# Entry of the experts in a vision tower: the shared expert's products moved ahead into the second norm, the router and the top-k

## The reference

```python
def _L0_ffn_ref(hidden_states, gate_w, Wg, Wu, Wd, Sg, Su, Sd):
    ...
    logits = flat_x @ gate_w.T
    scores = jax.nn.softmax(logits, axis=-1).T
    topk_weight, topk_idx = jax.lax.top_k(scores, C)
    xg = flat_x[topk_idx]
    ...
    sg = hidden_states @ Sg.T
    su = hidden_states @ Su.T
    shared = jax.nn.gelu(sg, approximate=False) * su @ Sd.T
    return out + shared
```

## Time and profile before

| | us |
|---|---|
| median of 3 runs | 865.48 (864.29 to 866.86) |
| the profiled execution's own time | 864.54 |
| its span, first to last instruction | 862.7 |
| PE busy (share of the span) | 798.5 (93%) |
| DVE busy | 642.3 (74%) |
| ACT busy | 462.2 (54%) |
| POOL busy | 256.9 (30%) |

### The profile page before, as it was taken

One profiled execution on the slowest core, in us unless ns is written; L12 is line 12 of the kernel. 1 busy time (PEld: TensorE's weight loads), 2 busy tenths in 40 slices (PEclk: granted clock), 3 DMA queues, 4 the chain that ended last, 5 costly groups with the idle time before them and its releaser, 6 DMA issues.

```text
span 862.7 us, 15969 instructions
## 1 busy us (share of the span) xinstructions
PE 798.5 (93%) x5736; PEld 731.1 (85%) x5736; DVE 642.3 (74%) x1285; ACT 462.2 (54%) x820; POOL 256.9 (30%) x297
## 2 busy tenths in 40 slices
PE   5889899999999997999999999989999998979698
PEld 4788769999999987898898979879897997969466
DVE  5696593877788768778778787877878787765686
ACT  3385314433333345776775777677567667725421
POOL 0002100411111101641654364164436516422232
PEclk9899799999999998899999999999999999988889
DMA  5000936988888702000210210021021002200000
GB/s 180 1 1 4 401 95 233 336 318 319 315 318 319 285 1 101 26 13 13 99 36 12 67 67 1 12 97 36 12 79 55 0 12 97 101 1 1 0 1 29
DMA packets 18289, 88.33 MB, mean 102 GB/s; under 512 B 3121, under 2 KB 7473, under 8 KB 12241
## 3 DMA queue, kind: packets, MB, share of 16 engines
q1 hardware_dynamic: 18256, 87.90, 28.8%
HBM read 85.05 MB, written 2.84 MB: 102 GB/s over the span
## 4 chain that ended last, share of the span: by engine, by line
PE 42%; issue 27%; POOL 18%; DVE 9%; ACT 3%; DMA 1%; POOLq 0%; SPq 0%; DVEq 0%; ACTq 0%
PE bank L1084 13%; POOL W_L L1903 6%; PE bank L1121 5%; POOL arena L1888 4%; POOL HF_L L1947 4%; PE bank L1226 3%; POOL WQKV_L L1903 2%; PE bank L770 2%; PE bank L724 2%; PE bank L1130 2%; POOL SQ L1917 2%; PE bank L1402 2%; PE bank L1067 1%; PE bank L872 1%; DVE CN L1991 1%
## 5 line engine op out<-in xcount | busy, mean ns | idle before, releaser
L1084 PE MATMUL bank<-arena 128*128 (+1 forms) x1024 | 117.9, 274 | 0.5 <-ACT arena L1646 0.5
L1084 PEld LDWEIGHTS bank<-arena 128*128 128x128 f32 x1024 | 117.4, 192 | 0.7 <-ACT arena L1646 0.7
L1888 POOL TENSOR_TENSOR arena<-arena,srec 111x456 f32<-111x456 f32 x56 | 52.4, 963 | 129.4 <-DVE srec L2047 129.4
L770 PE MATMUL bank<-XHL,W_H 128*128 128x296 f32 x384 | 90.2, 314 | 0.0
L770 PE MATMUL bank<-XHL,WQKV_H 128*128 128x296 f32 x288 | 73.1, 327 | 6.3 <-DVE XHL L2488 4.9
L1947 POOL TENSOR_TENSOR HF_L<-arena,HF_H 128x296 fp32r<-128x296 f32 x48 | 43.8, 935 | 111.5 <-ACT HF_H L1803 111.5
L1903 POOL TENSOR_TENSOR W_L<-LW,W_H 128x256 fp32r<-128x256 f32 x96 | 70.1, 772 | 18.9 <-ACT W_H L1689 18.9
L770 PEld LDWEIGHTS bank<-XHL,W_H 128*128 128x128 f32 x384 | 66.0, 194 | 1.2 <-DVE XHL L2488 1.2
L1803 ACT ACTIVATE arena<-bank,vec 128x296 f32<-128x296 f32 x96 | 48.8, 509 | 23.0 <-PE bank L770 22.4
L2059 DVE TENSOR_SCALAR OB<-bank,lvec 96x148 f32<-96x148 f32 x144 | 51.2, 368 | 12.8 <-PE bank L840 10.4
L770 PEld LDWEIGHTS bank<-XHL,WQKV_H 128*128 128x128 f32 x288 | 49.3, 192 | 13.2 <-DVE XHL L2488 8.0
(11 more groups left out here) (260 smaller groups left out, 2080.9 us busy)
## 6 DMA issues: line engine op xcount, KB each, us to landing
arena<-ew_in SPq DMA_DIRECT2D x16, 2048.0 KB, 9.3
arena<-ew_in SPq DMA_DIRECT2D x16, 1024.0 KB, 6.7
LW<-lw_in SPq DMA_DIRECT2D x12, 1024.0 KB, 4.9
arena<-route SPq DMA_DIRECT2D x32, 185.0 KB, 3.4
LW<-lw_in SPq DMA_DIRECT2D x6, 768.0 KB, 4.4
fp_weights<-arena SPq DMA_DIRECT2D x1, 2048.0 KB, 6.4
arena<-fp_weights SPq DMA_DIRECT2D x1, 2048.0 KB, 7.1
arena<-patches_in SPq DMA_DIRECT2D x2, 864.0 KB, 8.3
```

What stands on the lines that cost most here:

```text
L770: last = mm(o, w, x, start=(i == 0), stop=(i == len(pairs) - 1))
L1084: last = mm(o[:, m * CAP:(m + 1) * CAP], w[:, kc, mi * P:(mi + 1) * P], xg(kc, e), start=(kc == 0), stop=(kc == C - 1))
L1888: nc.gpsimd.tensor_tensor(v, v, srec[0:QROWS, s:s + 2, :].unsqueeze(3).to_broadcast([QROWS, 2, C * JH, KEYS]), ALU.mult).then_inc(p_ready, 1)
```

## The change

- The shared weights move within `LW`. Gate and up (`Ws_gu`) get a place that is free as soon as ACT has cast the last attention weight (`wo_cast`), and are loaded then. The down weights (`Ws_d`) are loaded once PE is through with the first attention products, on a semaphore of their own.
- On PE the gate half of pair 0 goes between the norm's mean and its variance, the up half of pair 0 between the norm's broadcast and the logits of tiles 2 to 4, and pair 1 between the logits and the score transposes. Logits of tiles 0 and 1 go behind the variance.
- All token transposes go behind the score transposes and write banks 6 and 7, in three groups with one copy each on ACT.
- Pairs 2 to 7 follow, with down products 0, 1 and 2 between them. The banks of the pairs are (2, 3), (4, 5), then (2, 3) and (0, 1) by turns. The score transposes write banks 0 and 1.
- On ACT the table of Exp is loaded behind the norm's root. Gelu of pair 0 goes ahead of the copy of the scores, Gelu of pair 1 behind it, and the copy `UT_H` behind Gelu of pair 2.

The core of the diff:

```diff
+        HS_AT, WS_AT = SM_ * D, SM_ * D + SM_ * N
+        Ws_d = LW[:, 0:HS_AT].rearrange("p (m n) -> p m n", m=SM_)
+        HS = LW[:, HS_AT:WS_AT].rearrange("p (m t) -> p m t", m=SM_)
+        Ws_gu = LW[:, WS_AT:WS_AT + 2 * C * SI].rearrange("p (g c n) -> p g c n", g=2, c=C)
+        SH_BANKS = ((2, 3), (4, 5)) + ((2, 3), (0, 1)) * (SM_ - 1)
...
+            sp.wait_ge(wo_cast, 1)
+            sp.dma_start(Ws_gu, a["ws_gu"]).then_inc(ld_sh, 16)
+            sp.wait_ge(filled["w"], nth("w", 3, 0))
+            sp.wait_ge(filled["r"], nth("r", 15, 0))
+            sp.dma_start(Ws_d, a["ws_d"]).then_inc(ld_shd, 16)
             sp.wait_ge(filled["p"], nth("p", 3, 0))
-            sp.dma_start(Ws_gu, a["ws_gu"]).then_inc(ld_sh, 16)
-            sp.dma_start(Ws_d, a["ws_d"]).then_inc(ld_sh, 16)
...
+            def shared_up(i, gs=(0, 1)):
+
+                m, h = i // 2, i % 2
+                if i >= 2 and gs[0] == 0:
+                    pe.wait_ge(sh_mul, max(j for j in range(i) if j == i - 2 or SH_BANKS[j] == SH_BANKS[i]) + 1)
+                for g in gs:
+                    for kc in range(C):
+                        last = mm(bank[SH_BANKS[i][g]][:, 0:NHALF], Ws_gu[:, g, kc, m * P:(m + 1) * P],
+                                  U[:, kc, h * NHALF:(h + 1) * NHALF], start=(kc == 0), stop=(kc == C - 1))
+                if gs[-1] == 1:
+                    last.then_inc(sh_psum, 1)
...
             ln_mean_of(LN_MOE, 1, ones_d)
+            pe.wait_ge(ld_sh, 16)
+            pe.wait_ge(u_ready, 1)
+            shared_up(0, (0,))
+            ln_var_of(LN_MOE, 1, ones_d)
             pe.wait_ge(ld_gate, 16)
-            pe.wait_ge(u_ready, 1)
             for t in range(2):
                 gate_logits(t)
-            turn_tokens(0)
-            ln_var_of(LN_MOE, 1, ones_d)
-            turn_tokens(1)
             ln_bcast_of(LN_MOE, 1)
+            shared_up(0, (1,))
             pe.wait_ge(u_ready, 2)
             for t in range(2, NT):
                 last = gate_logits(t)
             mark(last, "logits")
-            for t in range(2, NT):
-                turn_tokens(t)
-            pe.wait_ge(ld_sh, 32)
+            shared_up(1)
 
             pe.wait_ge(moe_dve, MOE_DVE["probs"])
...
             mark(last, "scoreT")
...
+            turn_tokens((0, 1))
+            turn_tokens((2, 3))
+            turn_tokens((4,))
+            shared_up(2)
             pe.wait_ge(moe_dve, MOE_DVE["scoreT"])
             pe.wait_ge(moe_act, MOE_ACT["scoreT"])
...
-            for kc in range(SM_ - 1):
-                shared_down(kc)
+            shared_up(3)
+            shared_up(4)
+            pe.wait_ge(ld_shd, 16)
+            pe.wait_ge(moe_act, MOE_ACT["ut4"])
+            shared_down(0)
+            shared_up(5)
+            shared_up(6)
+            shared_down(1)
+            shared_up(7)
+            shared_down(2)
             pe.wait_ge(moe_dve, MOE_DVE["pos"])
...
+            f(table_probe[:, :], eps1[:, :], ACT.Exp)
+            act.wait_ge(moe_dve, MOE_DVE["shift"])
+            mark(f(lg[:, 1], lg[:, 0], ACT.Exp), "exp")
+            shared_gelu(0)
+            act.wait_ge(moe_dve, MOE_DVE["scoreT"])
+            f(scoreT[0:E, 0:4 * P], bank[0][0:E, 0:4 * P], ACT.Copy)
+            mark(f(scoreT[0:E, 4 * P:N], bank[1][0:E, 0:N - 4 * P], ACT.Copy), "scoreT")
+            shared_gelu(1)
+            for tiles in ((0, 1), (2, 3), (4,)):
+                tokens_turned(tiles)
+            shared_gelu(2)
+            act.wait_ge(moe_act, MOE_ACT["ut4"])
+            f(UT_H, UT, ACT.Copy).then_inc(ut_lead, 1)
+            for i in range(3, 2 * SM_):
+                shared_gelu(i)
```

More of the change, by code:

```diff
@@ L1016, in _ @@
             mark(last, "logits")
-            for t in range(2, NT):
-                turn_tokens(t)
-            pe.wait_ge(ld_sh, 32)
+            shared_up(1)
             pe.wait_ge(moe_dve, MOE_DVE["probs"])
             for t in range(NT):
-                last = nc.tensor.transpose(bank[5 + t // 4][0:E, (t % 4) * P:(t % 4 + 1) * P],
-                                           lg[:, 2, t, :], ident)
+                last = nc.tensor.transpose(bank[t // 4][0:E, (t % 4) * P:(t % 4 + 1) * P], lg[:, 2, t, :], ident)
             mark(last, "scoreT")
[L1027 to L1039, removed]
+            turn_tokens((0, 1))
+            turn_tokens((2, 3))
+            turn_tokens((4,))
+            shared_up(2)
             pe.wait_ge(moe_dve, MOE_DVE["scoreT"])
             pe.wait_ge(moe_act, MOE_ACT["scoreT"])
[L1043 to L1047, removed]
-            for kc in range(SM_ - 1):
-                shared_down(kc)
+            shared_up(3)
[8 more added lines that the diff above has]
+            shared_down(2)
             pe.wait_ge(moe_dve, MOE_DVE["pos"])
@@ L1578, in _ @@
             keys_out(1)
-            f(WO0, w0_16[:, :, 5], ACT.Copy)
+            f(WO0, w0_16[:, :, 5], ACT.Copy).then_inc(wo_cast, 1)
             f(table_probe[:, :], eps1[:, :], ACT.Exp)
@@ L1617, in mark, with tokens_turned, shared_gelu @@
                 assert MOE_ACT[name] == done[0], (name, done[0])
-            def tokens_turned(t):
-                act.wait_ge(moe_pe, MOE_PE[f"ut{t}"])
-                mark(f(UT[:, t, :], bank[1 + t % 4][:, 0:D], ACT.Copy), f"ut{t}")
-            ln_square(LN_MOE, 1)
-            ln_root(LN_MOE, 1)
[L1625 to L1637, removed]
+            def tokens_turned(tiles):
+                act.wait_ge(moe_pe, MOE_PE[f"ut{tiles[0]}"])
+                o = bank[6 if tiles[0] != 2 else 7]
+                mark(f(UT[:, tiles[0]:tiles[-1] + 1, :],
+                       o[:, 0:len(tiles) * D].rearrange("p (t f) -> p t f", f=D), ACT.Copy), f"ut{tiles[0]}")
+            def shared_gelu(i):
                 act.wait_ge(sh_psum, i + 1)
@@ L1640, in _ @@
                     act.wait_ge(sh_mul, i - 1)
-                f(sh_ge[:, (i % 2) * NHALF:(i % 2 + 1) * NHALF], bank[i % 2][:, 0:NHALF], ACT.Gelu
+                f(sh_ge[:, (i % 2) * NHALF:(i % 2 + 1) * NHALF], bank[SH_BANKS[i][0]][:, 0:NHALF], ACT.Gelu
                   ).then_inc(sh_gelu, 1)
+            ln_square(LN_MOE, 1)
+            ln_root(LN_MOE, 1)
+            f(table_probe[:, :], eps1[:, :], ACT.Exp)
[13 more added lines that the diff above has]
+                shared_gelu(i)
             for i in range(8):
@@ L2733, in counts @@
     return out
-MOE_PE = counts(["ut0", "ut1", "logits", "ut2", "ut3", "ut4", "scoreT", "posT", "shared"] + [f"xg{i}" for i in range(8)])
-MOE_ACT = counts(["ut0", "ut1", "exp", "ut2", "ut3", "ut4", "scoreT"] + [f"xg{i}" for i in range(8)])
+MOE_PE = counts(["logits", "scoreT", "ut0", "ut2", "ut4", "posT", "shared"] + [f"xg{i}" for i in range(8)])
+MOE_ACT = counts(["exp", "scoreT", "ut0", "ut2", "ut4"] + [f"xg{i}" for i in range(8)])
 MOE_DVE = counts(["shift", "probs", "scoreT", "pos", "onehot0", "onehot1", "onehot2", "onehot3"])
```

31 lines of the change are left out of this document (19 added, 12 removed).

## The result

| | before | changed |
|---|---|---|
| median of 16 runs | 865.55 us | 870.03 us |
| range of the runs | 864.17 to 867.53 us (15 of 16) | 868.09 to 876.04 us |
| ratio | | 1.006, 95% interval 1.0045 to 1.0074 |
| profiled execution | 864.54 us, span 862.7 | 876.04 us, span 874.2 |

One run of the kernel before fell into a slow state (1004.64 us) and is left out of its range and of the ratio. The changed kernel is slower by 0.6%, 4.5 us between the medians. The forecast was 871.0, range 866.3 to 875.0. The profiled execution is the slowest of its 16, 6.0 us above their median, so its whole difference of 11.5 us must not be read as the change's. What can be read from it is the stretch that the change rewrites.

A forecast was written before the change was run, and what follows sets the result against it. It took the chain from the norm on PE through DVE's top-k to the gather, then PE in the experts, as the bound. Front 3.5, middle 1.0 and tail 2.0 added to 864.54 gave 871.0 us, range 866.3 to 875.0.

The forecast's parts named there:

- case A: Whole kernel: front, middle and tail sum to +6.5 us, giving 871.0 us; chance 0.65.
- Loads: nothing: Shared-weight loads: issued early with thirty microseconds of slack, they cost nothing.
- Front: +3.5: Norm to top-k: at clock 0.50 the moved products start the top-k 3.5 us later; at full clock -1.2.
- The broadcast's term: Norm's broadcast on PE: logits of tiles 0 and 1 behind the variance push it back by 0.3 us.
- rival B: Clock low for part of the front only: front -1.2 to +1.5, total 866.3 to 869.0 us; chance 0.20.
- First Gelu: -2.06: Start of the top-k: DVE's wait for the first Gelu before its first `HS` goes, saving 2.06 us.
- Middle: `HS` 5 late by 1.2, `HS` 7 by another 1.9: Top-k: two down products ahead of awaited pairs cost 3.1 us; with the first Gelu's saving, +1.0 net.
- Tail: +2.0, bounds 0 and 3.3: Behind PE's 5.5 us gap before the positions: low clock makes the fourth down product 2.0 us longer.
- ACT and POOL: nothing: ACT's copies and POOL's split of `UT`, moved behind Gelu 2, are wanted 20 us later and cost nothing.
- The experts take nothing back: Experts' loop, bound by PE: whatever delays the gather delays the end by the same amount.
- C: Clock full all through, the gap before the positions too: -0.2 us, 864.3 us; chance 0.08.
- D: DVE stays the pace of the whole top-k, jobs of 1.2 us or less: 861.2 us; chance 0.07.

The follow-up runs named there:

- late loads: Changed kernel with both loads of the shared weights back behind the last attention projection, pairs kept in their new places; median 876.24 us, ratio 1.0127.
- second profile: The changed kernel run and profiled once more, nothing altered; median 869.52 us, ratio 1.0068 against the kernel before.
- downs late: Changed kernel with down products 0 and 1 put behind pair 7 again; median 867.12 us, ratio 1.0008.
- best version: Changed kernel with logits 0, 1 before variance, pair 0's up half behind logits, pair 1 behind score transposes, downs behind pair 7, eight unused records in gap; 0.9982, 0.9978.
- pair 1 late: Changed kernel with pair 1 moved behind the score transposes; median 869.99 us, ratio 1.0077.
- filled gap: Changed kernel with 20 records of unused products added behind down product 2, in PE's gap before the positions; median 868.56 us, ratio 1.0038.
- pair 1 and downs late: Changed kernel with pair 1 behind the score transposes and down products 0 and 1 behind pair 7; run twice, 863.43 and 865.45 us, ratios 0.9976 and 1.0002.
- logits ahead: Changed kernel with logits 0 and 1 before variance, pair 0's up half behind logits, pair 1 behind score transposes, downs behind pair 7; 865.57 us, ratio 1.0017.

## Why the prediction was right

The median of 870.03 is the 871.0 of case A, less 1.0. By its steps:

- *Loads: nothing.* Right. The landing at 59.5 and the absence of any wait for it show it, and the late loads show what they would have cost. Nor did the transfers slow what runs beside them (below).
- *Front: +3.5, the low end of the clock taken.* In the profiled execution 16.53 - 13.24 = +3.3, with the parts as they were put: half a pair in 1.97, then pair 1 in 4.07 and the score transposes right behind it at 105.38, not with the softmax. The top-k stands at 106.89 and not near the 102.4 forecast, because the mean itself starts 4.71 later; without that it is 102.2. The broadcast's term was +0.3 and measured +0.7 against the mean, since the clock had fallen already. In the second profile the front was +1.6. The mechanism holds in both, and with the downs late in either case moving pair 1 shortens the front by 2.19, the +2.1 of its term; the size of the whole hangs on where in the front the clock falls. The step took one end. The ratio's 0.6% are 5.2 us (3.9 to 6.4); less 1.1 for the middle and 3.0 for the tail they leave 1.1 for the front (1.9, where the tail costs only 2.2), so a typical execution seems nearer to rival B's +1.5. That last step is worked out, not seen in a trace.
- *First Gelu: -2.06.* Right: no wait, `HS` 0 at T + 1.68. And it is the gain that the best version keeps.
- *Middle: `HS` 5 late by 1.2, `HS` 7 by another 1.9.* Measured 1.22 and 1.92, the last `HS` at T + 19.08 for 19.0. The kernel with the downs late shows the cause, since without the two down products it is T + 16.01. The size is exact because the clock was full there in both executions (1.00 from 109.1 to 127.3 and from 106.0 to 124.3), so a job is 2.0 us, and the count decides.
- *Tail: +2.0, bounds 0 and 3.3.* This is a term that was mis-sized: 3.07 and 2.99 (2.2 and 2.5 behind the same gap in the kernels with the loads and with pair 1 late). The prediction took the down product alone at half speed and the gather at full again. The clock stayed low for longer: in the chain the down product took 4.24 instead of 2.19, the gather 11.72 instead of 10.93, and the transposes before them 0.2 more. That it was the clock, the filled gap shows.
- *ACT and POOL: nothing.* Right for the change.
- *The experts take nothing back.* Right.

The sum of the parts in the profile is 3.3 + 1.1 + 3.1 = +7.4 (6.5 forecast), and in the second 1.6 + 1.1 + 3.0 = +5.7, against 4.5 between the medians. Front too high and tail too low cancelled in part, and the sum was added to a profiled execution 1.0 below the median before: a forecast of +6.5 stands against a measured +4.5 to +5.2, and part of the closeness of 871.0 to 870.0 is luck. Two small sums were off as well: the three additions to 871.0 give 875.2 for the upper end and not 875.0, and of B's range a third lies above 868.1, not two fifths.

The rest of the 11.5 us between the profiled executions lies ahead of the stretch: the mean starts 4.7 later. It isn't the change's. ACT's cast, behind which the moved load is first issued, already stands 3.4 later than in the earlier trace rows:

```profile
53.83 0.61 ACT L1598 ACTIVATE LW<-LW 128x512 f32<-128x512 f16 x1
```

From this cast to the mean, the time in which the moved loads run, it is 35.2 us before the change and 35.2 in eight of the eleven profiles with the early loads. In the other three it is 36.5 to 38.1, and in the kernel with the loads late, 36.5. So the early loads cost nothing that shows. Over the eleven the mean starts anywhere from 84.97 to 90.36.

Of the rivals, B describes the front of the second execution (14.88 - 13.24 = +1.6, just above its +1.5), but its total had the tail at 2.0 too. C is refuted: the gap cost clock. D too: DVE was not the pace of the top-k, since the jobs took 2.0 us each and not 1.2. The Trainium skill's rule that the prediction weighed (page "TensorE: Matmul & The Clock Gate", section "Why this matters for your kernels": keep TensorE busy between bursts, avoid long gaps) held in one of the two directions. The gap of 5.3 us cost 3 us, and work put into it for no other end gave them back; the trace agrees there, and the gaps of 2.07 us show that shorter ones than the section warns of can cost too. In the front it gave nothing that a run shows: the norm's gaps were filled, and the clock was 0.50 all the same for 10.3 us in which PE had no idle time. And the products that went into the earlier gaps came out of the later place, and so opened the gap there.

Still open: what sets where the clock falls in the front, and how long it stays low behind the 5.29 us gap; why the two runs of "pair 1 and downs late" differ by 0.26% with equal stretches; and why the kernel with the logits ahead, 0.3 us below the kernel before in the stretch, measured 1.0017 (its median is 0.15 us below that of the kernel before). The last two are about the size of their intervals.

## What to carry to other kernels

When work moves within one engine's ordered list, write the list down with absolute times and read off when each waited-for result leaves it; adding up local savings counted the first Gelu's 2 us and would have missed the 3 us behind it. Never put work that nobody waits for yet (here the down products) ahead of work that someone does. And ask of each move what fills the place it leaves: a gap on PE may cost the clock of what follows.

## What was not expected of the hardware

- **DVE beside POOL.** The `TENSOR_SCALAR` of 16x592 took 0.46 us in the other kernels and 1.42 where POOL's `TENSOR_TENSOR` of 128x1280 (116.36 to 119.25) ran beside it, ending 0.33 behind POOL's end. `MAX8` (0.77) and `MATCH_REPLACE8` (0.76), in the same 2.9 us, kept their times. The Trainium skill, page "SBUF — State Buffer", section "SBUF: two separate sides", says that DVE and GpSimd share one pair of ports under an exclusive lock, so that the one who comes second waits for the whole instruction of the first. By the page this goes for a DVE instruction in a two-port performance mode, or with two inputs in SBUF against a GpSimd instruction that reads SBUF. The trace agrees for this instruction; in which mode it ran, no run shows.
- **The clock behind a short gap.** Gaps of 2.07 us before the positions were followed by 0.59 over 4.0 us in one kernel and by 0.51 over 3.3 in another; gaps of 1.58 us, in two profiles of a third, were not. In these four profiles what PE did ahead was the same, pairs and then down products without a pause. (The gap of 1.8 us before the change was not followed by a low clock either, but it stood between the pairs and the down products.) Four executions make no bound. In the tail the low stretch is worth 1.6 us, as much as the mended list had won.
- **A busy engine at the low clock.** In the front PE worked without idle time at 0.50 for 10.3 us (17.4 with late loads). Work put in front of waited-for work there costs double (pair 1: 4.07 us for a job of 2.0).
